# Attention row maxima from two heads side by side in 64-row tiles, with exps and outputs taken by halves of the queries

## The chip, the cores and the metric

The kernel runs on one core of one Trainium2 chip. A core has a matrix engine (TensorE, PE in the rows), a vector engine (DVE), a scalar engine (ACT), a general engine (GpSimd, POOL) and a sync engine (SP) that here issues DMAs. Each engine works through its own list of instructions in order and waits on semaphores that the others raise. The metric is the device time of the whole program in microseconds (us), the median of several runs; lower is better.

## The reference, cut to what matters

Two layers run over 4 batches of 1024 tokens of width 256: expert feed-forward, causal softmax attention, expert feed-forward, quantized feed-forward, linear attention, quantized feed-forward. The change is in the softmax attention, with 16 heads of width 16:

```python
qkv = (x @ W_qkv.T).reshape(B, L, 3, H, dk)      # B=4, L=1024, H=16, dk=16
attn = jnp.einsum('bhqd,bhkd->bhqk', q, k) * scale
attn = jnp.where(causal, attn, -jnp.inf)
attn = jax.nn.softmax(attn, axis=-1)
y = jnp.einsum('bhqk,bhkd->bhqd', attn, v)
```

## The kernel before, in words

`attention_phase` runs 16 iterations, one for each batch and group of four heads. q and k were written to DRAM as three bf16 parts each (high, middle, low), so that sums of part products come close to fp32. `load_block` reads them back as stacks: `sq` and `sk` hold, for each head, six blocks of 16 rows (96 rows, `SROWS`). Block r multiplies part `QROWS[r]` of q with part `KROWS[r]` of k, and one matmul over the 96 rows adds all six products:

```python
QROWS, KROWS = (0, 0, 1, 1, 0, 2), (0, 1, 0, 1, 2, 0)
```

Every score is computed twice.

- S pieces (`score_s`, L1351): queries on the partitions, keys along the row, over 96 rows. They serve for the row maxima alone. On the diagonal a second matmul (L1357, 128 rows) adds a large negative number where the key lies after the query. DVE takes the maximum over each piece (`reduce`, L1429). A piece fills at most one PSUM bank of 512 columns, and `psS` is a ring of three banks.
- E pieces (`score_e`, L1373): keys on the partitions, queries along the row, over 98 rows: 96 of the stack, and two that hold the negated maximum as two bf16 parts in `sq` against ones in `sk`. ACT takes the exponential into `PT` (L1485), POOL clears the triangle of the diagonal tile (L1332), and `weigh` (L1389) multiplies `PT` with the values in fp32, four heads in four 32-column tiles of the array, into `psO` (two banks). ACT copies `psO` out by halves (L1493), PE turns it (L1404), DVE divides.

An iteration has 38 S pieces and 38 E pieces. Each kind covers 4608 columns in each head, 18432 in all. The masks of the diagonal cover another 4096.

The order is written out by hand in `order`: E pieces go by key tile (`kt`), each over both halves of the queries; after every E piece stands one S piece of the next iteration, nine pieces ahead (`LEAD`). `weigh` of a key tile comes three pieces after its last E piece, so there are eight in an iteration. Ahead of the loop stand all S pieces of the first iteration and nine of the second. When the last S piece of an iteration has been reduced, DVE negates and splits the maxima, PE turns them (L1397), DVE copies them to `maxT` (L1451), and SP writes them into the spare rows of `sq` with two DMAs (L1295); the first E piece of the iteration waits for these. SP also loads the stacks two iterations ahead, with 12 DMAs of 128 KB each (L959).

Of the kernel before, what the change touches and what calls it, by code (L numbers as in the profile page):

```python
# [13 lines left out]
BF16 = mybir.dt.bfloat16  # L14
# [674 lines left out]
def experts(nc, st, sem, tag, ctx, r, psT, psH, psY, fp4=None, ring=TILES):  # L689
# [136 lines left out]
    def vector(dve):  # L826
# [30 lines left out]
        def set_spare_rows(t, p):  # L857

            if t < len(st.sk):
                dve.memset(st.sk[t][SROWS:P, :, :], 1.0)  # L860
# [328 lines left out]
def attention_phase(nc, st, sem, tag):  # L1189
# [5 lines left out]

    names = "s_filled s_drained e_filled e_drained maxed weighted o_out inverted v_set padded cleared spared".split()
# [3 lines left out]
    KROW = SROWS + 2  # L1200
    MAX = 4
    RING = 3
    LEAD = 9
    LAG = 3
    HALF = BT // 2

    s_pieces = []
# [6 lines left out]
    for kt in range(BT):  # L1214
        for c in range(kt // HALF, 2):
            n = (c + 1) * 512 - max(kt * P, c * 512)
            e_pieces += [(kt, c, n, h, 512 // n) for h in range(0, HG, 512 // n)] if n != 384 else \
                        [(kt, c, n, h, 1) for h in range(HG)]
    S, E = len(s_pieces), len(e_pieces)
    assert S == E  # L1220
    last_diagonal = [max(j for j, piece in enumerate(e_pieces) if piece[:2] == (kt, kt // HALF)) for kt in range(BT)]
    last_e = [max(j for j, piece in enumerate(e_pieces) if piece[0] == kt) for kt in range(BT)]
    turn_slot = S - 1 - LEAD + 3

    def order(it):

        if it < 0:
            for u in range(S + LEAD):
                yield "s", u // S, u % S
                if u == S + 2:  # L1230
                    yield "max", 0, 0
            return
        for j in range(E if it < ITS else 8):
            if it < ITS:
                yield "e", it, j
            u = (it + 1) * S + LEAD + j
            if u < ITS * S and it < ITS:
                yield "s", u // S, u % S
            if j == turn_slot and it + 1 < ITS:
                yield "max", it + 1, 0  # L1240
            for kt in range(BT):
                due = last_e[kt] + LAG
                if due < E and j == due and it < ITS:
                    yield "weigh", it, kt
# [1246 lines left out]
```

## Time and profile before

| what | value |
| --- | --- |
| median of 3 runs | 2176.65 us (2174.5 to 2178.46) |
| profiled execution, whole | 2175.08 us |
| profiled execution, span | 2173.4 us |
| PE / DVE / ACT / POOL busy | 2031.1 / 1467.3 / 1018.7 / 922.0 us |
| attention | about 437 to 937 us of the span |

The span is the time between the first and the last instruction of one profiled execution; 1.7 us of that execution lie outside it. Attention takes some 500 us of it. In the middle of that stretch the work of one iteration repeats exactly, so that a difference for one iteration can be multiplied by the number of iterations. The recorded length of a matmul includes the time that its results take to leave the array; the distance between the starts of neighbouring matmuls tells what one costs.

### The profile page before, as it was taken

The numbers are of one execution on the slowest core, as the hardware profiler recorded it, in microseconds if no ns is written. First come the engines' busy times: TensorE is split into PE (matmuls) and PEld (weight loads), VectorE is DVE, ScalarE is ACT, GpSimd is POOL, SyncE is SP. The second block draws the span as 40 slices with busy tenths as digits, with TensorE's granted clock in tenths as the row PEclk, the third lists the DMA queues.
The fourth block names the chain that finished last, engine by engine and source line by source line (L and its number), as shares of the span: only waits on it lengthen the run. The fifth ranks groups of instructions, "written<-read, shape, count | busy, mean of one in ns | idle before, by whom it ended". The sixth has DMA issues, their size and how long they took to land.

```text
span 2173.4 us, 41823 instructions
## 1 busy us (share of the span) xinstructions
PE 2031.1 (93%) x13717; PEld 1414.7 (65%) x13717; DVE 1467.3 (68%) x4020; ACT 1018.7 (47%) x2367; POOL 922.0 (42%) x1139
## 2 busy tenths in 40 slices
PE   6899999899999999977899998999989999799998
PEld 5899996534444444357799995666756666566676
DVE  4443555388888888535775358989866666588884
ACT  4333333336666666743433333333346666433332
POOL 4323655421111111214323555555556666455553
PEclk9899999969999999998999999999999999999999
DMA  5456663544443444012456652000000000000000
GB/s 185 172 193 213 229 211 119 164 59 60 60 50 50 51 60 60 2 41 95 161 184 213 234 187 51 0 0 0 1 1 2 2 2 2 2 11 17 12 20 20
DMA packets 101710, 173.58 MB, mean 80 GB/s; under 512 B 14704, under 2 KB 66320, under 8 KB 101520
## 3 DMA queue, kind: packets, MB, share of 16 engines
q1 hardware_dynamic: 95376, 154.40, 27.0%
q0 software_dynamic: 6144, 16.79, 2.4%
q8 instruction: 102, 1.67, 0.3%
q14 instruction: 88, 0.72, 0.1%
HBM read 136.01 MB, written 34.87 MB: 79 GB/s over the span
## 4 chain that ended last, share of the span: by engine, by line
PE 35%; DVE 11%; issue 5%; POOL 2%; ACT 2%; DVEq 0%; DMA 0%; POOLq 0%; SPq 0%; ACTq 0%
PE s_HH L785 5%; PE s_Y L797 4%; PE s_Y L1851 4%; PE s_R L1821 3%; PE s_HH L1821 3%; PE s_HH L2173 3%; PE s_R L2160 1%; PE s_R L452 1%; PE s_R L2208 1%; PE s_Y L2244 1%; PE s_Y L2252 1%; PE s_R L2194 1%; DVE ff_hscale L1534 1%; DVE fw_down L1537 1%; DVE s_HH L1714 1%
## 5 line engine op out<-in xcount | busy, mean ns | idle before, releaser
L1429 DVE TENSOR_REDUCE a_part_max<-a_psS 128x1 f32<-128x512 f32 (+3 forms) x608 | 362.6, 654 | 76.2 <-PE a_psS L1357 67.5
L1485 ACT ACTIVATE a_PT<-a_psE 128x512 f32<-128x512 f32 (+1 forms) x608 | 309.3, 584 | 175.9 <-PE a_psE L1373 159.0
L1332 POOL TENSOR_SCALAR_AFFINE_SELECT a_PT<-a_PT 128x512 f32<-128x512 f32 x128 | 81.2, 634 | 399.0 <-ACT a_PT L1485 399.0
L1764 POOL TENSOR_TENSOR fw_down<-fw_down,ff_hm 128x704 f32<-128x704 f32 x64 | 97.3, 1520 | 250.3 <-DVE fw_down L1546 250.3
L1851 PE MATMUL s_Y<-w_down,fw_up 128*128 128x256 f32 x768 | 181.0, 386 | 22.6 <-ACT fw_up L1801 20.9
L1786 ACT ACTIVATE ff_hm<-fw_down 128x704 bf16<-128x704 f32 x64 | 50.6, 790 | 279.7 <-DVE fw_down L1537 279.7
L1851 PEld LDWEIGHTS s_Y<-w_down,fw_up 128*128 128x128 f32 x768 | 143.7, 191 | 47.5 <-ACT fw_up L1801 30.5
L1821 PE MATMUL s_R<-w_gate,ff_xqT 128*128 128x512 f32 (+1 forms) x512 | 164.6, 465 | 4.8 <-ACT ff_sil L1796 4.8
L1821 PE MATMUL s_HH<-w_up,ff_xqT 128*128 128x512 f32 (+1 forms) x512 | 163.0, 462 | 3.6 <-DVE fw_down L1537 2.4
L1389 PE MATMUL a_psO<-a_PT,a_va 128*32 128x512 f32 (+3 forms) x1536 | 150.4, 494 | 2.5 <-POOL a_PT L1332 1.8
L1351 PE MATMUL a_psS<-a_sk,a_sq 96*128 96x512 bf16 (+2 forms) x480 | 144.0, 335 | 1.9 <-DVE a_part_max L1429 0.3
L1373 PE MATMUL a_psE<-a_sq,a_sk 98*128 98x512 bf16 (+3 forms) x480 | 140.6, 328 | 0.0
L785 PE MATMUL b_H<-e_xsT,e_w 128*128 128x128 f32 x1120 | 136.3, 281 | 0.0
L1821 PEld LDWEIGHTS s_R<-w_gate,ff_xqT 128*128 128x128 f32 x512 | 90.1, 193 | 67.4 <-issue 67.3
L797 PE MATMUL s_Y<-wo_moe,e_gT 128*128 128x256 f32 x560 | 129.2, 384 | 4.4 <-DVE e_y L844 2.5
L785 PE MATMUL s_HH<-e_xsT,e_w 128*128 128x128 f32 x1120 | 133.3, 278 | 0.0
L785 PEld LDWEIGHTS b_H<-e_xsT,e_w 128*128 128x128 f32 x1120 | 133.1, 198 | 0.1
L1821 PEld LDWEIGHTS s_HH<-w_up,ff_xqT 128*128 128x128 f32 x512 | 89.3, 191 | 66.0 <-issue 61.4
L785 PEld LDWEIGHTS s_HH<-e_xsT,e_w 128*128 128x128 f32 x1120 | 130.3, 195 | 0.1
L797 PE MATMUL b_Y<-wo_moe,e_gT 128*128 128x256 f32 x560 | 127.8, 381 | 0.0
L797 PEld LDWEIGHTS s_Y<-wo_moe,e_gT 128*128 128x128 f32 x560 | 104.9, 193 | 17.8 <-issue 2.7
L1990 POOL TENSOR_SCALAR_AFFINE_SELECT V<-V 128x512 f32<-128x512 f32 x128 | 78.0, 643 | 88.2 <-ACT V L2129 88.2
(484 smaller groups left out, 4308.6 us busy)
## 6 DMA issues: line engine op xcount, KB each, us to landing
e_w<-w_in SPq DMA_DIRECT2D x70, 1024.0 KB, 5.0
e_xs<-sorted_x SPq DMA_DIRECT2D x70, 128.0 KB, 3.5
e_xr<-sorted_x SPq DMA_DIRECT2D x70, 128.0 KB, 4.4
sorted_y<-e_yo SPq DMA_DIRECT2D x70, 128.0 KB
a_sq<-qk_parts SPq DMA_DIRECT2D x60, 128.0 KB, 6.5
a_sk<-qk_parts SPq DMA_DIRECT2D x60, 128.0 KB, 7.1
sq<-qk_parts SPq DMA_DIRECT2D x36, 128.0 KB, 5.8
sk<-qk_parts SPq DMA_DIRECT2D x36, 128.0 KB, 6.4
```

The lines of the kernel that those rows point to most:

```text
L785: mm = pe.matmul(psH[half][:, n * P:(n + 1) * P], w1[p][:, k, c * P:(c + 1) * P], xsT[p][:, k, :], start=k == 0, stop=k == KD - 1)
L797: mm = pe.matmul(psY[:, 0:D], gT[p][:, k, :], st.wo_moe[:, k, :], start=k == 0, stop=k == KI - 1, skip_group_check=True)
L1332: pool.affine_select(out=hidden, in_=hidden, compare_op=ALU.is_ge, fill=0.0, base=0, pattern=[[0, HG], [1, P]], channel_multiplier=-1).the ...
L1351: mm = pe.matmul(out[:, i * n:(i + 1) * n], sq[it % 3][0:SROWS, h0 + i, qt * P:(qt + 1) * P], sk[it % 3][0:SROWS, h0 + i, c * 512:c * 512 ...
L1373: mm = pe.matmul(out[:, i * n:(i + 1) * n], sk[it % 3][0:KROW, h0 + i, kt * P:(kt + 1) * P], sq[it % 3][0:KROW, h0 + i, q0:q0 + n], start= ...
L1389: mm = pe.matmul(psO[32 * h:32 * h + 32, q0:(c + 1) * 512], va[it % 2][:, kt, h, :], PT[kt % 2][:, h, q0:(c + 1) * 512], start=kt == 0, st ...
L1429: dve.tensor_reduce(part_max[:, c, h0:h0 + heads, qt], psS[place % RING][:, 0:heads * n].rearrange("p (h k) -> p h k", h=heads), AX.X, ALU ...
L1485: act.activation(PT[kt % 2][:, h0:h0 + heads, q0:q0 + n], psE[e % RING][:, 0:heads * n].rearrange("p (h q) -> p h q", h=heads), ACT.Exp, s ...
L1764: c.link(pool.tensor_tensor(hv[i], hv[i], hm[i][:], ALU.subtract))
L1821: mm = pe.matmul(out[:, a:b], xqT[p % 2][:, k, :], w[:, k, a:b], start=k == 0, stop=k == KD - 1)
L1851: mm = pe.matmul(psY[:, 0:D], hqT[p % 2][:, k, :], st.w_down[:, k, :], start=k == 0, stop=k == KF - 1)
L1990: pool.affine_select(out=a, in_=a, compare_op=ALU.is_ge, fill=0.0, base=0, pattern=[[0, 4], [1, P]], channel_multiplier=-1).then_inc(clear ...
```

## The change

- The stack is laid out anew for heads 2 and 3 of a group. Heads 0 and 1 keep their blocks in rows 0 to 95. Heads 2 and 3 have blocks 0 to 3 in rows 64 to 127 and blocks 4 and 5 in rows 32 to 63; their two rows of maxima are rows 0 and 1, and rows 0 to 31 are otherwise zeros in `sq` against ones in `sk`. Each DMA of a block is split in two (24 of 64 KB in an iteration), and so is each DMA of maxima (four of them).
- S pieces use blocks 0 to 3 alone, 64 rows: head h in rows 0 to 63, head h + 2 in rows 64 to 127, each with a matmul of its own, into two neighbouring banks. An iteration has 20 S pieces of up to 1024 columns, one DVE maximum goes over both banks, and `psS` is a ring of two pairs. The masks still use 128 rows.
- E pieces go by half of the queries (c) and then by key tile, and there are 12 groups of them (4 for the first half, 8 for the second). `weigh` is done for each group, 12 in an iteration, into one output bank that both halves use in turn. `PT` is a ring of four half-width tiles. E pieces of heads 2 and 3 are over 128 rows.
- An S piece is placed where the width of the E pieces so far calls for it (`s_due`), five pieces ahead.

```diff
+def stack_row(half, r):
+    return (r if half == 0 else r + 4 if r < 4 else r - 2) * HD
...
-        sp.dma_start(stack[it % 3][r * HD:(r + 1) * HD, :, :], src).then_inc(st.stacked[it % 3], 16)
+        for half in (0, 1):
+            row, heads = stack_row(half, r), slice(2 * half, 2 * half + 2)
+            sp.dma_start(stack[it % 3][row:row + HD, heads, :], src[:, heads, :]).then_inc(st.stacked[it % 3], 16)
...
-    RING = 3
-    LEAD = 9
+    PAIRS, RING, WEIGHTS = 2, 3, 4
+    LEAD = 5
...
-            s_pieces += [(qt, c, n, h, 512 // n) for h in range(0, HG, 512 // n)] if n != 384 else \
-                        [(qt, c, n, h, 1) for h in range(HG)]
+            s_pieces += [(qt, c, n, 0, 2)] if n <= 256 else [(qt, c, n, h, 1) for h in (0, 1)]
+    groups = [(c, kt) for c in (0, 1) for kt in range(HALF * (c + 1))]
...
+                for k in range(due[j - 1] if j else 0, due[j]):
+                    u = (it + 1) * S + LEAD + k
+                    if u < ITS * S:
+                        yield "s", u // S, u % S
...
-                for i in range(heads):
-                    mm = pe.matmul(out[:, i * n:(i + 1) * n],
-                                   sq[it % 3][0:SROWS, h0 + i, qt * P:(qt + 1) * P],
-                                   sk[it % 3][0:SROWS, h0 + i, c * 512:c * 512 + n],
-                                   start=i == 0, stop=not diagonal, skip_group_check=True)
+                for i in range(per):
+                    for half in (0, 1):
+                        rows, head = slice(64 * half, 64 * half + 64), 2 * half + h + i
+                        mm = pe.matmul(out[:, half, i * n:(i + 1) * n],
+                                       sq[it % 3][rows, head, qt * P:(qt + 1) * P],
+                                       sk[it % 3][rows, head, c * 512:c * 512 + n],
+                                       start=i == 0, stop=not diagonal, skip_group_check=True)
...
-                for c in range(kt // HALF, 2):
-                    q0 = max(kt * P, c * 512)
-                    for h in range(HG):
-                        mm = pe.matmul(psO[32 * h:32 * h + 32, q0:(c + 1) * 512], va[it % 2][:, kt, h, :],
+                q0 = max(kt * P - c * 512, 0)
+                for h in range(HG):
+                    mm = pe.matmul(psO[32 * h:32 * h + 32, q0:512], va[it % 2][:, kt, h, :],
...
-                dve.tensor_reduce(part_max[:, c, h0:h0 + heads, qt],
-                                  psS[place % RING][:, 0:heads * n].rearrange("p (h k) -> p h k", h=heads),
+                dve.tensor_reduce(part_max[:, c, :, qt].rearrange("p (b h) -> p b h", b=2)[:, :, h:h + per],
+                                  psS[place % PAIRS][:, :, 0:per * n].rearrange("p b (h k) -> p b h k", h=per),
```

PE's list before, in the middle of an iteration, between two `weigh`s (`a_psO`). `a_psE` are E pieces, `a_psS` S pieces, and `ident_bf` marks the mask:

```order
L1389 MATMUL a_psO<-a_PT0,a_va1 32x512 x4
L1373 MATMUL a_psE2<-a_sq2,a_sk2 128x512
L1351 MATMUL a_psS2<-sk0,sq0 128x512
L1357 MATMUL a_psS2<-hide_k_after_q,ident_bf 128x128
L1373 MATMUL a_psE0<-a_sq2,a_sk2 128x512
L1351 MATMUL a_psS0<-sk0,sq0 128x512
L1357 MATMUL a_psS0<-hide_k_after_q,ident_bf 128x128
L1373 MATMUL a_psE1<-a_sq2,a_sk2 128x512
L1351 MATMUL a_psS1<-sk0,sq0 128x512
```

The same place in the changed kernel, where L1409 is the E piece, L1385 the S piece and L1392 the mask:

```order
L1428 MATMUL a_psO<-a_PT2,a_va0 32x512 x4
L1409 MATMUL a_psE2<-sq0,sk0 128x512
L1385 MATMUL a_psS0<-a_sk1,a_sq1 128x512 x2
L1392 MATMUL a_psS0<-hide_k_after_q,ident_bf 128x128 x2
L1409 MATMUL a_psE0<-sq0,sk0 128x512
L1409 MATMUL a_psE1<-sq0,sk0 128x512
L1385 MATMUL a_psS1<-a_sk1,a_sq1 128x512 x2
L1392 MATMUL a_psS1<-hide_k_after_q,ident_bf 128x128 x2
L1409 MATMUL a_psE2<-sq0,sk0 128x512
```

An S piece is now two matmuls over 64 rows each (`x2`), and it stands between matmuls over 98 or 128 rows. Most have an E piece ahead of them and an E piece or a mask behind.

The second place is where the four `weigh`s of one half of the queries come close together. Before, around the last two `weigh`s of an iteration:

```order
L1389 MATMUL a_psO<-a_PT0,a_va1 32x256 x4
L1373 MATMUL a_psE2<-sq0,sk0 128x512
L1351 MATMUL a_psS1<-a_sk1,a_sq1 128x512
L1389 MATMUL a_psO<-a_PT1,a_va1 32x128 x4
L1373 MATMUL a_psE0<-sq0,sk0 128x512
L1351 MATMUL a_psS2<-a_sk1,a_sq1 128x512
```

Now, in the first half of the queries of an iteration, a place that had no counterpart:

```order
L1428 MATMUL a_psO<-a_PT1,a_va0 32x384 x4
L1409 MATMUL a_psE2<-sq0,sk0 128x512
L1385 MATMUL a_psS1<-a_sk1,a_sq1 128x512 x2
L1409 MATMUL a_psE0<-sq0,sk0 128x512
L1428 MATMUL a_psO<-a_PT2,a_va0 32x256 x4
L1409 MATMUL a_psE1<-sq0,sk0 128x512
L1385 MATMUL a_psS0<-a_sk1,a_sq1 128x256 x4
```

Such a run of narrow `weigh`s now comes twice in an iteration, once for each half.

## Rows read from the trace of the kernel before

**Rows 1.** The page: busy time of each engine; the span in 40 slices.

```profile
PE 2031.1 (93%) x13717; PEld 1414.7 (65%) x13717; DVE 1467.3 (68%) x4020; ACT 1018.7 (47%) x2367; POOL 922.0 (42%) x1139
PE   6899999899999999977899998999989999799998
```

**Rows 2.** Stretches of attention: us, busy of each engine, PE clock, DMA share.

```profile
449.00:453.00 4.00, 4.00 (x12) 1.04 (x11) 4.00 (x8) 0.00 (x0) 0.00 (x0) 0.50 0.40 46
620.00:680.00 60.00, 59.64 (x452) 25.40 (x450) 49.51 (x96) 40.83 (x83) 11.26 (x18) 1.00 0.46 55
925.00:930.00 5.00, 4.28 (x33) 1.09 (x25) 0.00 (x0) 3.69 (x8) 0.19 (x2) 1.00 0.00 2
```

**Rows 3.** Timeline, DVE: the copy of the maxima, one in an iteration.

```profile
609.85 0.20 DVE L1451 COPY a_maxT<-a_psS 64x128 bf16<-64x128 bf16 x1
639.51 0.20 DVE L1451 COPY a_maxT<-a_psS 64x128 bf16<-64x128 bf16 x1
```

**Rows 4.** Timeline, PE: an S piece and an E piece of 512 columns.

```profile
624.89 0.38 PE L1351 MATMUL a_psS<-sk,sq 96*128 96x512 bf16 x1
625.11 0.38 PE L1373 MATMUL a_psE<-a_sq,a_sk 98*128 98x512 bf16 x1
```

**Rows 5.** Timeline, PE: two `weigh`s (1024 and 640 columns a head) and their neighbours.

```profile
621.43 0.39 PE L1351 MATMUL a_psS<-sk,sq 96*128 96x512 bf16 x1
621.75 1.92 PE L1389 MATMUL a_psO<-a_PT,a_va 128*32 128x512 f32 x16
623.61 0.34 PE L1373 MATMUL a_psE<-a_sq,a_sk 98*128 98x384 bf16 x1
...
636.33 1.28 PE L1389 MATMUL a_psO<-a_PT,a_va 128*32 128x128 f32 x16
637.55 0.39 PE L1373 MATMUL a_psE<-a_sq,a_sk 98*128 98x512 bf16 x1
```

**Rows 6.** Timeline, PE and its weight loads: between 128 rows and 48.

```profile
1066.45 0.23 PE L593 MATMUL s_R<-r_numbers,ones_bf 128*128 128x128 bf16 x1 [3.11 <-DVE r_match_bf L640]
1066.61 0.23 PE L594 MATMUL s_R<-r_match_bf,r_numbers 48*128 48x128 bf16 x1
1066.77 0.70 PE L797 MATMUL s_Y<-wo_moe,e_gT 128*128 128x256 f32 x2
...
1061.27 0.10 PEld L588 LDWEIGHTS s_R<-r_diagonals,ones_bf 128*128 128x128 bf16 x1
1061.27 1.88 PEld L785 LDWEIGHTS s_HH<-e_xsT,e_w 128*128 128x128 f32 x16
```

**Rows 7.** Timeline, PE: linear attention, four 32-row tiles side by side, and fp32 transposes.

```profile
1699.96 0.41 PE L2278 MATMUL s_HH<-ident,e_gT 128*128 128x128 f32 x2 [0.21 <-issue]
1700.29 1.15 PE L2160 MATMUL s_R<-e_w,e_gT 32*128 32x256 f32 x16
1701.37 1.98 PE L2173 MATMUL s_HH<-lin_w,e_gT 128*128 128x512 f32 x4
...
1705.14 0.60 PE L2218 MATMUL s_R<-ident,e_w 128*128 128x128 f32 x4
1705.58 0.60 PE L2230 MATMUL s_HH<-ident,V 128*128 128x128 f32 x4
```

**Rows 8.** DVE maxima: groups by shape (busy, mean ns, idle before), timeline of five.

```profile
L1429 DVE TENSOR_REDUCE a_part_max<-a_psS 128x1 f32<-128x512 f32 x384 | 241.7, 681 | 26.7 <-PE a_psS L1357 19.0 <-PE a_psS L1351 7.8
L1429 DVE TENSOR_REDUCE a_part_max<-a_psS 128x1 f32<-128x384 f32 x128 | 65.9, 547 | 30.2 <-PE a_psS L1357 30.2
...
443.38 3.07 DVE L1429 TENSOR_REDUCE a_part_max<-a_psS 128x1 f32<-128x512 f32 x5
```

**Rows 9.** Maxima: DMA issues, a pair of them on SP, the first E piece behind.

```profile
a_sq<-a_maxT SPq DMA_DIRECT2D x20, 8.0 KB, 1.9
463.07 1.30 SPq L1295 DMA_DIRECT2D sq<-a_maxT  x2
...
644.14 0.39 PE L1373 MATMUL a_psE<-sq,sk 98*128 98x512 bf16 x1
```

More of the change, by code:

```diff
@@ L1210, in attention_phase, with s_due @@
             n = min(512, (qt + 1) * P - c * 512)
-            s_pieces += [(qt, c, n, h, 512 // n) for h in range(0, HG, 512 // n)] if n != 384 else \
-                        [(qt, c, n, h, 1) for h in range(HG)]
+            s_pieces += [(qt, c, n, 0, 2)] if n <= 256 else [(qt, c, n, h, 1) for h in (0, 1)]
+    groups = [(c, kt) for c in (0, 1) for kt in range(HALF * (c + 1))]
     e_pieces = []
-    for kt in range(BT):
-        for c in range(kt // HALF, 2):
[L1216 to L1223, printed above, removed]
+    for c, kt in groups:
+        n = (c + 1) * 512 - max(kt * P, c * 512)
+        e_pieces += [(c, kt, n, h, 512 // n) for h in range(0, HG, 512 // n)] if n != 384 else [(c, kt, n, h, 1) for h in range(HG)]
+    S, E, GR = len(s_pieces), len(e_pieces), len(groups)
+    last_e = {g: max(j for j, piece in enumerate(e_pieces) if piece[:2] == g) for g in groups}
+    group_at = {g: i for i, g in enumerate(groups)}
+    s_width, e_width = [n * per for _, _, n, _, per in s_pieces], [n * heads for _, _, n, _, heads in e_pieces]
+    s_of = lambda k: s_width[(LEAD + k) % S]
+    turn_slot = S - 1 - LEAD + 2
+    def s_due(j):
+        share, k = sum(e_width[0:j + 1]) * sum(s_width) / sum(e_width), 0
+        while k < S and sum(s_of(i) for i in range(k + 1)) <= share + 1e-6:
+            k += 1
+        return k
+    due = [s_due(j) for j in range(E)]
+    assert due[-1] == S
     def order(it):
@@ L1235, in order @@
                 yield "e", it, j
[L1236 to L1244, printed above, removed]
-                elif due >= E and j == due - E and it > 0:
-                    yield "weigh", it - 1, kt
-            if j == last_e[HALF - 1] + LAG + 2 and it < ITS:
-                yield "out", it, 0
-            if j == last_e[BT - 1] + LAG - E + 2 and it > 0:
-                yield "out", it - 1, 1
-            if j == last_e[HALF - 1] + LAG + 5 and it < ITS:
-                yield "turn", it, 0
-            if j == last_e[BT - 1] + LAG - E + 5 and it > 0:
-                yield "turn", it - 1, 1
+                for k in range(due[j - 1] if j else 0, due[j]):
+                    u = (it + 1) * S + LEAD + k
+                    if u < ITS * S:
+                        yield "s", u // S, u % S
+                    if k == turn_slot and it + 1 < ITS:
+                        yield "max", it + 1, 0
+            for g in groups:
+                at = last_e[g] + LAG
+                if at < E and j == at and it < ITS:
+                    yield "weigh", it, g
+                elif at >= E and j == at - E and it > 0:
+                    yield "weigh", it - 1, g
+            for c in (0, 1):
+                for what, later in (("out", 1), ("turn", 4)):
+                    at = last_e[c, HALF * (c + 1) - 1] + LAG + later
+                    if at < E and j == at and it < ITS:
+                        yield what, it, c
+                    elif at >= E and j == at - E and it > 0:
+                        yield what, it - 1, c
     def whole():
@@ L1355, in score_s @@
                 if diagonal:
-                    at = out[:, 0:heads * n].rearrange("p (h k) -> p h k", h=heads)[:, :, n - P:n]
-                    mm = pe.matmul(at, st.ident_bf[:], st.hide_k_after_q[:].unsqueeze(1).broadcast_to([P, heads, P]),
-                                   start=False, stop=True, skip_group_check=True)
+                    for half in (0, 1):
+                        at = out[:, half, 0:per * n].rearrange("p (h k) -> p h k", h=per)[:, :, n - P:n]
+                        mm = pe.matmul(at, st.ident_bf[:], st.hide_k_after_q[:].unsqueeze(1).broadcast_to([P, per, P]),
+                                       start=False, stop=True, skip_group_check=True)
@@ L1359, in score_s @@
                 mm.then_inc(s_filled, 1)
             def score_e(it, j):
-                kt, c, n, h0, heads = e_pieces[j]
+                c, kt, n, h0, heads = e_pieces[j]
                 e = it * E + j
@@ L1456, in divide @@
                 dve.wait_ge(s_filled, place + 1)
[L1457 removed]
+                o = psS[place % PAIRS][:, 0, :].rearrange("p (t h w) -> p t h w", t=HALF, w=32)
                 dve.reciprocal(inverse[c][:], o[:, :, :, HD]).then_inc(inverted, 1)
```

107 lines of the change are left out of this document (59 added, 48 removed).

## The prediction, made before the changed kernel ran

> **What bounds the kernel now.** I read the page first. PE is busy 93% of the span and at 8 or 9 tenths in nearly every slice; DVE is at 68% [rows 1]. The change is inside attention, so the second view is the busy time by stretches. In the middle of attention PE is busy 59.64 us of 60, DVE 49.51, ACT 40.83, POOL 11.26, and PE's clock is granted in full [rows 2]. A busy PE is not a PE at its peak, so the third view is the timeline. One iteration lasts 639.51 - 609.85 = 29.66 us, from one copy of the maxima to the next [rows 3].
>
> What fills these 29.66 us I add up from the starts of neighbouring matmuls.
> - 512 bf16 columns cost 0.22 us from start to start [rows 4], in finer terms 512 / 2.4 GHz = 0.213. E pieces: 18432 columns, 36 x 0.213 = 7.7 us. S pieces: the same, 7.7. Masks: 4096 columns, 1.7.
> - `weigh` of 1024 columns a head takes 623.61 - 621.75 = 1.86 us and of 640 columns 637.55 - 636.33 = 1.22 [rows 5]. The difference, 0.64 us for 384 columns, is 0.213 for 128: four passes over each column, with the four heads side by side. 1024 columns are then 1.71 us, and 0.15 is left over. Ahead of it stands an S piece that needs 0.213 and has 0.32 [rows 5], so 0.11 more. Each `weigh` thus costs some 0.25 us beside its columns. Eight of them: 4608 x 4 / 2400 = 7.7 us, and 8 x 0.25 = 2.0.
> - Turning the output: eight fp32 transposes, four of which take 0.44 [rows 7], 0.9; the maxima 0.05.
>
> Sum 27.8. The other 1.8 us are small stalls of PE, for the most part on DVE: its maximum over 512 columns takes 0.598 us from start to start ((3.07 - 0.68) / 4), more than the 0.43 of an S and an E piece, and only the `weigh`s let it catch up [rows 8]. So PE bounds an iteration, with DVE close behind.
>
> **The change, part by part.** Per iteration, at the full clock.
>
> 1. S pieces over 64 rows, two heads at once. That two heads in different rows run together is to be seen in linear attention: 16 instructions of 256 fp32 columns (two passes each, 0.213 us) over 32 rows took 1701.37 - 1700.29 = 1.08 us, where one after the other would need 3.4 and four at a time 0.85 [rows 7]. For pairs: 7.7 -> 3.85, a gain of 3.85 us. The masks stay at 1.7, since both heads still need their columns.
>
> 2. What stands against it is the change of tile. Between a matmul over 128 rows and one over 48 the weight load doesn't go ahead: starts are 0.16 us apart both ways (1066.45, 1066.61, 1066.77) for 128 columns that need 0.053, so 0.107 each way. Between two matmuls over 128 rows the next load starts with the one before (both at 1061.27), and costs nothing [rows 6]. The 96 and 98 rows of today are of that second kind [rows 4]. The 64-row pieces stand in 20 places, and all are entered and left through another shape; two are followed by a `weigh`, which has paid for a change anyway. Price of one place: the two changes alone, 0.21 (below it, nothing, if 64 rows behaved as 96 do); with four tiles filled in turn, 0.25 at `weigh` [rows 5]; with 32-row fp32 tiles (0.33 - 0.21) + (1.08 - 0.85) = 0.35 [rows 7]. I take 0.25, because it is in the middle, and has several tiles to fill: 20 x 0.25 - 2 x 0.11 = 4.8 us. Bounds 4.0 and 6.8.
> The Trainium skill says the same of the change of tile (TensorEngine Tiling (Array Packing), Key Properties): changing the tiling mode, not just the tile, drains TensorE. It speaks against this change, since with it the pieces alternate between modes. The trace agrees for 48 and 32 rows; no row has exactly 64. By that rule the sum is as here; by the page's "up to 2x" alone it would be that of rival B.
>
> 3. Twelve `weigh`s for eight: 4 x 0.25 = 1.0 us more. The columns are the same.
>
> 4. DVE: the same columns, 18 instructions fewer. The means of 681 ns for 512 columns and 547 for 384 give 1.05 ns a column [rows 8]; 512 of them are 0.536, so 0.06 us goes with each instruction. DVE has 18 x 0.06 = 1.1 us less to do. Its ring holds two pairs of 1024 columns, in columns as much as today or a little more. PE's stalls of 1.8 us can fall to nothing or stay. Between two `weigh`s a piece of E, E and S is 0.43 + 0.21 + 0.25 = 0.9 us of PE, against 1.13 us of DVE (2 x 0.536 + 0.06): DVE is still the slower one there, though by less. I take 1.2 us of stalls.
>
> 5. The maxima go by four DMAs in place of two. Today the first E piece comes 644.14 - 639.51 = 4.6 us after the copy [rows 3, 9]; copy, two issues (1.30 us for a pair) and 1.9 us to landing make 3.4, so 1.2 us is to spare. Two more issues take 1.1 to 1.3, and the copy may stand behind one maximum of 1.13 us. What PE waits there lies between 0 and 1.2; I take 0.6. Everything on PE behind this E piece waits, S pieces too.
>
> 6. One output bank. The first `weigh` of a half waits until ACT has copied the half before. Between them PE has four or five E pieces and two S pieces (some 2 us), against one exp and the copy, some 0.6 each. Hidden; if not, 0.3 us twice an iteration, which is inside the range. ACT has 40.83 of 60 us to do [rows 2], and its work is the same. POOL also.
>
> 7. The stacks are loaded by 24 DMAs of 64 KB for 12 of 128, two iterations ahead: the same bytes, at 0.46 of the DMA engines [rows 2]. Hidden. Ahead of the loop DVE bounds PE (4.00 of 4.00 busy at half the clock) [rows 2]; 25 pieces for 47 save 22 x 0.06 = 1.3 us. The memsets of the spare rows are done by POOL in that time.
>
> Sum of an iteration: E 7.7, S 3.85, masks 1.7, `weigh` 7.7 + 12 x 0.25 = 10.7, turns 0.95, changes of tile 4.8, stalls 1.2, wait for the maxima 0.6: 31.5 us, against 29.66. That is 1.84 more, for the 15 iterations that hold both E and S pieces 27.6 us. The last has no S pieces: about 1 more, for its four `weigh`s. Ahead of the loop 1.3 less. Together +27. The profiled execution took 2175.08 us; 2202. It is 1.6 under the median of the runs, so I say 2203.
>
> **The rivals.**
>
> A, the forecast. The changes of tile and the added `weigh`s (5.8) eat more than the pair gains (3.85). Its own range: 0.21 and 0.35 for a place give 30.7 to 33.5 us an iteration, 2190 to 2234.
>
> B, the other side: no change of tile between 128 and 64 rows. A place then costs the filling of its second tile at most, for which I take half of a weight load, 0.05. Columns and `weigh`s of the sum above are 24.9 us, the places 1.0. DVE now needs 36 x 0.536 + 20 x 0.06 = 20.5 us for the maxima and some 2.4 for the rest, so that stalls stay near today's 1.8; the wait for the maxima stays at 0.6. Together 28.3 us, 1.36 less than today, 20 us in 15 iterations: 2155. It decides from the price of a place at which the gain is gone: 0.25 - 1.84 / 20 = 0.16 us. For it: no row has 64 rows, and the 96-row pieces run without a gap. Against it: four changes in a row between 128 and 48 rows, and those at 32. Chance 0.25.
>
> C, the pairs don't run side by side, or at a price like 0.4 a place. S stays at 7.7 with the changes on top: 3.85 more in an iteration, less the stalls of 1.2, which a slower PE hides: 2.65 x 15 = 40 on the forecast, 2243. Against it the four tiles at once in [rows 7]. Chance 0.08.
>
> D, the clock. Ahead of the loop PE is granted half its clock although it is busy 4.00 of 4.00, with every S piece waiting for DVE; in the loop, with matmuls end to end, it is granted the whole, and it keeps it at the end of attention, with 4.28 of 5 busy [rows 2]. In the changed loop a quarter of the time is changes of tile (4.8 + 3.0 of 31.5), so the rise from half the clock could come later. An iteration at half the clock costs the columns once more, 22 us. One such: 2225; all sixteen: some 2550. Chance 0.07, nearly all for the first.
>
> E, no difference: the terms cancel within 0.2%, 4 us. Chance 0.07.
>
> **The numbers.** A has 0.53. Slower by over 0.2% (about what a measurement of this kernel can tell from none) hold A, C and D: 0.68. Faster: B, 0.25. The same: 0.07. The range is to hold 8 in 10: the better half of B and the upper end of A with most of C, 2156 to 2242. A alone: 2190 to 2234.
>
> **What the profile after should show.** A period of 31 to 32 us between copies of the maxima. The S pieces of a pair starting together, or within 0.1 us. Around them weight loads that start only when the columns before have gone through, 0.1 us lost on either side; an E piece behind an E piece with none. DVE busy some 22 us of an iteration. A short wait of the first E piece on the maxima's DMA. The forecast is wrong if the load of a 64-row piece starts during the E piece before it (B), if the second head of a pair starts 0.2 us after the first (C), or if PE's clock is at half beyond the first few microseconds of the loop (D).

## The result

The changed kernel took 2193.22 us in the median of four runs (2188.8 to 2199.99), the kernel before, run beside it, 2177.47 (2174.5 to 2178.46, four runs). The ratio is 1.0076, with a 95% interval from 1.0063 to 1.009: slower by 15.75 us. The forecast was 2203. Its sign was right, and its step was too large: it had +27 us.

The profiled execution of the changed kernel is the longest of the four (2199.99 us), so that I compare iterations and stages, not whole spans. The page first, its busy times and the slices [rows 1]:

```profile
PE 2023.8 (92%) x13701; PEld 1374.7 (63%) x13749; DVE 1458.4 (66%) x3734; ACT 1029.0 (47%) x2367; POOL 926.0 (42%) x1143
PE   6899999889999999877899998999989999799998
PEclk9899999979999999988999999999999999999999
```

PE shows less busy time in a longer span. Its digit has fallen from 9 to 8 in the 9th and the 17th slice, where attention's loop begins and ends; in the middle tenths are too coarse. The stretches say it more finely [rows 2]: length, busy time of PE, weight loads, DVE, ACT, POOL, then PE's clock, DMA share and GB/s.

```profile
469.00:473.00 4.00, 3.66 (x20) 0.95 (x19) 3.13 (x3) 2.83 (x6) 0.64 (x1) 0.74 0.49 138
473.00:477.00 4.00, 4.00 (x40) 1.64 (x37) 2.83 (x4) 2.81 (x6) 2.25 (x4) 1.00 0.50 143
620.00:680.00 60.00, 56.83 (x442) 19.35 (x440) 46.81 (x58) 40.68 (x80) 10.76 (x18) 1.00 0.20 54
```

PE is busy 56.83 us of 60 where it was 59.64. DVE is busy 46.81, which makes 23.7 us in an iteration (24.5 before). The granted clock comes to its full level, 2.4 GHz, at about 471 us, and stays there to the end of attention. The stacks' many small DMAs have not cost anything that I can see: the DMA engines' share is 0.20, where it was 0.46.

One iteration, from one copy of the maxima to the next [rows 3], with what SP and PE do behind it [rows 9]:

```profile
647.32 0.20 DVE L1490 COPY a_maxT<-a_psS 64x128 bf16<-64x128 bf16 x1
647.55 2.41 SPq L1323 DMA_DIRECT2D sq<-a_maxT  x4
651.18 0.61 PE L1409 MATMUL a_psE<-sq,sk 98*128 98x512 bf16 x2 [0.24 <-DMA sq<-a_maxT]
...
677.75 0.20 DVE L1490 COPY a_maxT<-a_psS 64x128 bf16<-64x128 bf16 x1
```

It lasts 30.43 us (29.66 before). Four issues take 2.41 us where a pair took 1.30. The first E piece, 3.86 us behind the copy, found its maxima 0.24 us late here; in some iterations it is 0.8 to 1.7, and those last 31 to 31.9 us. Over the fifteen iterations from 463.46 to 922.66 the mean is 30.61 (29.48 before), and without the first and the last of them, which are of another length in every kernel, 30.69. Attention begins at 438.08 us and ends (first matmul of the next stage) at 955.8, where it began at 437.37 and ended at 939.25: it takes 15.8 us longer, and this is the difference of the medians too. Of these, 17.0 lie between the first and the last copy of the maxima; up to the first copy it is 0.1 less, and behind the last one 1.1 less. The other 8.3 us by which this profiled execution is longer lie behind attention, where the two programs are the same. That part took 1233 to 1242 us in the profiled executions of this document, so a difference of a few us between medians says less than one between periods.

The place of a 64-row piece, in the timeline of PE and its weight loads:

```profile
648.62 0.10 PEld L1385 LDWEIGHTS a_psS<-a_sk,a_sq 64*128 64x128 bf16 x2 [0.21 <-issue]
648.62 0.34 PE L1385 MATMUL a_psS<-a_sk,a_sq 64*128 64x384 bf16 x2
648.88 0.11 PEld L1392 LDWEIGHTS a_psS<-hide_k_after_q,ident_bf 128*128 128x128 bf16 x2 [0.17 <-issue]
648.89 0.29 PE L1392 MATMUL a_psS<-hide_k_after_q,ident_bf 128*128 128x128 bf16 x2
648.96 0.49 PEld L1409 LDWEIGHTS a_psE<-a_sq,a_sk 128*128 128x128 bf16 x6
649.01 0.61 PE L1409 MATMUL a_psE<-a_sq,a_sk 128*128 128x256 bf16 x6
649.55 0.39 PE L1385 MATMUL a_psS<-a_sk,a_sq 64*128 64x512 bf16 x2
649.87 0.29 PE L1392 MATMUL a_psS<-hide_k_after_q,ident_bf 128*128 128x128 bf16 x2
```

Two heads of 384 columns stand in one row of two matmuls, and what follows starts 0.27 us later: 384 columns at 2.4 GHz are 0.16, and 0.11 is left for the change of tile. With 512 columns it is 0.32, so 0.21 and again 0.11. The two heads do run side by side. The loads of the 64-row piece, and of the mask behind it, start with their own matmuls: they have gone ahead of nothing. The load behind a mask, for an E piece over 128 rows (648.96), goes ahead by 0.05 us. On the way in it is 0.11 too: the six E matmuls at 649.01 are 1024 columns, which need 0.43 us and have 0.54. So a place costs 0.215 us, the lower bound of the forecast's range, and the second tile costs nothing that adds to it.

DVE's side [rows 8], by shapes, between 560 and 800 us (busy, mean ns, idle before):

```profile
L1468 DVE TENSOR_REDUCE a_part_max<-a_psS 128x2 f32<-128x1024 f32 x95 | 113.3, 1222 | 32.2 <-PE a_psS L1392 16.0 <-PE a_psS L1385 15.6
L1468 DVE TENSOR_REDUCE a_part_max<-a_psS 128x2 f32<-128x768 f32 x30 | 27.4, 954 | 8.5 <-PE a_psS L1392 8.5
```

And the waits of that stretch, us in total, times, longest:

```profile
PEld a_psE L1409 <- ACT a_PT L1522: 31.3, 52, 0.8
...
DVE a_part_max L1468 <- PE a_psS L1385: 15.6, 24, 0.7
...
PEld a_psS L1385 <- DVE a_part_max L1468: 10.5, 36, 0.4
```

DVE waits for PE to fill a pair of banks, and PE waits for DVE to empty one: each holds the other up, and neither is busy all the time. How much of this is due to the banks standing in pairs, these rows don't tell.

### The profile page after: what moved, and what is told of

Its sections match the earlier page's. It is cut to its first block, busy times and chain, and to the rows that moved or that the text cites. A ratio compares the mean times of both kernels' runs of the same rounds, so it can differ in the third digit from the quotient of the medians.

```text
span 2198.2 us, 41804 instructions
## 1 busy us (share of the span) xinstructions
PE 2023.8 (92%) x13701; PEld 1374.7 (63%) x13749; DVE 1458.4 (66%) x3734; ACT 1029.0 (47%) x2367; POOL 926.0 (42%) x1143
## 4 chain that ended last, share of the span: by engine, by line
PE 36%; DVE 10%; issue 5%; ACT 2%; POOL 2%; DMA 0%; DVEq 0%; POOLq 0%; SPq 0%; ACTq 0%
PE s_HH L785 5%; PE s_Y L797 5%; PE s_Y L1887 4%; PE s_HH L1857 3%; PE s_R L1857 3%; PE s_HH L2209 3%; PE s_R L452 2%; PE s_R L2196 1%; PE s_R L2244 1%; PE s_Y L2280 1%; PE s_Y L2288 1%; PE s_R L2230 1%; DVE ff_hscale L1570 1%; DVE fw_down L1573 1%; DVE s_HH L1750 1%
## 5 line engine op out<-in xcount | busy, mean ns | idle before, releaser
L1468 DVE TENSOR_REDUCE a_part_max<-a_psS 128x2 f32<-128x1024 f32 (+2 forms) x320 | 346.8, 1115 | 95.5 <-PE a_psS L1392 65.3
L1522 ACT ACTIVATE a_PT<-a_psE 128x512 f32<-128x512 f32 (+1 forms) x608 | 319.2, 579 | 181.5 <-PE a_psE L1409 176.5
L1428 PE MATMUL a_psO<-a_PT,a_va 128*32 128x512 f32 (+3 forms) x1536 | 163.6, 497 | 12.6 <-ACT a_PT L1522 5.3
L797 PEld LDWEIGHTS s_Y<-wo_moe,e_gT 128*128 128x128 f32 x560 | 105.7, 194 | 20.1 <-issue 4.0
L1409 PE MATMUL a_psE<-a_sq,a_sk 98*128 98x512 bf16 (+7 forms) x450 | 111.6, 326 | 4.9 <-DMA a_sq<-a_maxT 4.3
L821 ACT ACTIVATE e_gT<-b_H,e_bias 128x128 f32<-128x128 f32 x280 | 79.6, 369 | 77.0 <-PE b_H L785 77.0
```

The source lines that it names most:

```text
L797: mm = pe.matmul(psY[:, 0:D], gT[p][:, k, :], st.wo_moe[:, k, :], start=k == 0, stop=k == KI - 1, skip_group_check=True)
L821: ins = act.activation(gT[p][:, c, :], psH[half][:, n * P:(n + 1) * P], ACT.Gelu, bias=bias[p][:, c:c + 1])
L1409: mm = pe.matmul(out[:, i * n:(i + 1) * n], sk[it % 3][rows, h0 + i, kt * P:(kt + 1) * P], sq[it % 3][rows, h0 + i, q0:q0 + n], start=i == ...
L1428: mm = pe.matmul(psO[32 * h:32 * h + 32, q0:512], va[it % 2][:, kt, h, :], PT[(it * GR + group_at[g]) % WEIGHTS][:, h, q0:512], start=kt == 0,
L1468: dve.tensor_reduce(part_max[:, c, :, qt].rearrange("p (b h) -> p b h", b=2)[:, :, h:h + per], psS[place % PAIRS][:, :, 0:per * n].rearran ...
L1522: act.activation(PT[group % WEIGHTS][:, h0:h0 + heads, q0:512], psE[e % RING][:, 0:heads * n].rearrange("p (h q) -> p h q", h=heads), ACT.Exp,
```

## The experiments

Two things are to be told apart: what PE has to do by itself (columns, changes of tile, `weigh`s), and how long it stands because of the others. For each kernel I read the period in the middle of attention. PE's own work is the sum of the forecast, 27.8 us for the kernel before, with the terms that the runs below measured; the rest of the period I call stalls.

**x2_halves.** The kernel before, with only the other part of the change: exps by halves, four buffers of weights, twelve `weigh`s, one output bank. Score pieces as before.

```diff
-        PT = [sb(f"PT{i}", [P, HG, SEQ]) for i in (0, 1)]
+        PT = [sb(f"PT{i}", [P, HG, 512]) for i in range(WEIGHTS)]
...
-        psO = ps("psO", [P, SEQ])
+        psO = ps("psO", [P, 512])
...
-                for c in range(kt // HALF, 2):
-                    q0 = max(kt * P, c * 512)
+                q0 = max(kt * P - c * 512, 0)
```

> The kernel before with only the second part of the change: exps by halves of the queries, twelve weighs in place of eight, one output bank, PT as four half tiles. S pieces, ring and stacks as before. T: 4 more weighs at 0.25 us, 1.0 us an iteration, 2177 + 16 = 2193 (2188 to 2197). R: PE's stalls on DVE (1.8 us an iteration) absorb it: 2175 to 2182.

2182.62 us (ratio 1.0026, interval 1.0011 to 1.004): 0.6 above the rival's range and 5 below the theory's. The period is 29.82 us, 0.16 more than before:

```profile
641.76 0.21 DVE L1454 COPY a_maxT<-a_psS 64x128 bf16<-64x128 bf16 x1
671.58 0.21 DVE L1454 COPY a_maxT<-a_psS 64x128 bf16<-64x128 bf16 x1
```

Yet the four more `weigh`s do cost PE their price. A `weigh` of 512 columns takes 1.0 us from its start to the next, with 0.85 of columns, and the piece ahead of it has lost 0.1; that is the forecast's 0.25. PE's own work is 28.8 us. The stalls have fallen from 1.9 to 1.0. From 560 to 800 us the loads of the S pieces wait 20.1 us for DVE's maxima in the kernel before, and 10.3 us here. That this comes of the shorter `weigh`s, which hold up the others less, is my reading; no run varies it alone.

**x1_one_tile.** The changed kernel, its S pieces over 96 and 128 rows, one head after the other: no change of tile, nothing side by side; banks in pairs, maxima by four DMAs, order and halves as in the changed kernel. (A wait for the spare rows is added in iterations 1 and 2.)

```diff
...
-                        rows, head = slice(64 * half, 64 * half + 64), 2 * half + h + i
+                        rows, head = slice(0, SROWS if half == 0 else P), 2 * half + h + i
```

> The changed kernel, with its S pieces over 96 rows (heads 0 and 1) and 128 rows (heads 2 and 3) in place of 64, so that no tile is changed and the two heads of a pair run one after the other; order, banks and maxima as in the changed kernel. For heads 2 and 3 the extra rows add old maxima to the scores and the two low products. Theory T (a change of tile costs PE 0.107 us, 40 of them in an iteration, and that eats what the pairs gain): the pairs' 3.85 us an iteration come back as cost, the 4.1 of changes go, so within 5 us of the changed kernel's 2193: 2185 to 2197. Rival R (the changes are absorbed in waits for DVE; the loss comes from the ring of two pairs and the late maxima): nothing goes, 3.85 us an iteration are added, less what hides in stalls: 2225 to 2250.

2197.67 us (ratio 1.01, 1.0078 to 1.0121), just above the theory's range and far from the rival's. The period is 30.46, that of the changed kernel:

```profile
558.79 0.20 DVE L1492 COPY a_maxT<-a_psS 64x128 bf16<-64x128 bf16 x1
589.25 0.21 DVE L1492 COPY a_maxT<-a_psS 64x128 bf16<-64x128 bf16 x1
```

So the pairs side by side and their changes of tile, taken together, moved the period by nothing. And without either of them the kernel was already 0.8 us an iteration slower than before, 0.64 slower than x2_halves, which has the same work for PE. This I had not forecast. I had put the whole loss on the changes of tile and the added `weigh`s. In one period PE stands three times, for three others:

```profile
562.66 0.61 PE L1411 MATMUL a_psE<-sq,sk 98*128 98x512 bf16 x2 [0.22 <-DMA sq<-a_maxT]
585.16 0.39 PE L1387 MATMUL a_psS<-a_sk,a_sq 96*128 96x128 bf16 x4 [0.21 <-DVE a_part_max L1470]
588.57 1.06 PE L1430 MATMUL a_psO<-a_PT,a_va 128*32 128x512 f32 x8 [0.28 <-ACT a_PT L1524]
```

Together 0.71 us, where PE stands 0.11 in all in a period of x2_halves. One of the three is the wait for a pair of banks; the others are the maxima's DMA and a `weigh` that comes close behind its exps. x1_one_tile differs from x2_halves in the banks, in the order of the pieces and in the DMAs at once, so the 0.64 us are not divided among these by any run.

**x6_doubled.** The changed kernel with each S piece of more than 256 columns a head cut in two, an E piece between the parts: 16 more places, the same columns. Five of the new places are followed by a `weigh` and two stand behind one, which pays for a change anyway. Counted in the two lists, PE changes shape 87 times in an iteration where it did 62: 25 more.

```diff
+                lo, hi = (0, n) if per == 2 else (256, n) if second else (0, 256)
...
-                        mm = pe.matmul(out[:, half, i * n:(i + 1) * n],
+                        mm = pe.matmul(out[:, half, i * n + lo:i * n + hi],
```

> The changed kernel, with each S piece of 384 or 512 columns (16 of the 20) done in two parts, columns 0 to 255 and the rest, with an E piece between them: the same columns and maxima, some 14 to 16 more places where the tile is changed and changed back. T: 15 x 0.215 = 3.2 us an iteration, less up to 1 that hides in stalls: 2193 + 35 to 50 = 2228 to 2243. R: 2193 to 2205.

2246.16 us (ratio 1.033, 1.0311 to 1.0349), slightly above the range of the theory.

```profile
702.06 0.20 DVE L1509 COPY a_maxT<-a_psS 64x128 bf16<-64x128 bf16 x1
...
735.97 0.21 DVE L1509 COPY a_maxT<-a_psS 64x128 bf16<-64x128 bf16 x1
```

33.91 less 30.43 is 3.48 us. Of these, 25 changes at 0.107 are 2.7. The other 0.8 are waits: PE stands more for DVE's maxima in this period (0.58, 0.31 and 0.22 us) than in the changed kernel's (0.22).

```profile
713.20 0.29 PE L1400 MATMUL a_psS<-a_sk,a_sq 64*128 64x128 bf16 x4 [0.58 <-DVE a_part_max L1487]
723.13 0.28 PE L1400 MATMUL a_psS<-a_sk,a_sq 64*128 64x256 bf16 x2 [0.31 <-DVE a_part_max L1487]
```

3.48 over 16 places is 0.218 each, as if it were the timeline's 0.215 again, but this is a coincidence. What the run shows is that the price of a change of tile is real, that no stall absorbs it, and that it lies between 0.107 and 3.48 / 25 = 0.139 us. The Trainium skill has it as a drain when the tiling mode changes (TensorEngine Tiling (Array Packing), Key Properties). Forecast and rule stand, with 0.107 us each way at the full clock.

**x4_lead6** and **x0_mask_first.** The maxima's DMA, and the order inside a piece. The first starts the S pieces of an iteration one piece earlier (`LEAD = 6` for 5); the second adds the masks ahead of the scores, not behind them:

```diff
+                if diagonal and masks:
...
+                                  start=True, stop=False, skip_group_check=True)
-                                       start=i == 0, stop=not diagonal, skip_group_check=True)
+                                       start=i == 0 and not diagonal, stop=True, skip_group_check=True)
```

> The changed kernel with S pieces six ahead in place of five, so that the maxima are turned one piece (1.5 us) earlier against the first E piece. T: that piece no longer waits for the DMAs, 0.3 to 1.2 us an iteration: 2193 - 4 to 15 = 2178 to 2189, and the period is even at about 30.1. R (the wait only moves to DVE): 2190 to 2196.

> The changed kernel, with the mask of a diagonal piece written ahead of its scores and the scores added to it. The mask then joins the E piece before it, and the places at which the tile is changed stay as many. Theory T (0.107 us for each change of tile, on PE's path): the same as the changed kernel, a period of 30.4 us, 2188 to 2198. Rival R (what costs is the ring of two pairs, which the mask holds up): the same too; this run is the base of the next two.

x4_lead6: 2192.19 us (ratio 1.0078, 1.0061 to 1.0095), the rival. Every iteration lasts 30.47 us (30.1 had been expected), the uneven ones are gone, and the attention stage ends at 952.5, 3.3 us earlier than in the profiled execution of the changed kernel. The median moved by 1 us, within its uncertainty. Behind the first iteration no E piece waits for the maxima any more, but PE stands elsewhere, where it turns them:

```profile
612.52 0.23 PE L1436 MATMUL a_psS<-ident_bf,a_max_bf 128*128 128x128 bf16 x1 [0.75 <-DVE a_part_max L1468]
```

So the late maxima cost at most a few us. The forecast had 0.6 x 15 = 9. x0_mask_first, a single run, 2190.77 us: the period is 29.97 in its plain iterations (615.38 to 645.35), 0.46 less, and the stage ends at 950.8. The expectation had as many changes of tile as before, and that was wrong: with the masks ahead, six S pieces end in their scores right before a `weigh`, where two did, so PE changes shape 58 times for 62. Four changes are 0.43 us, which is nearly all of the 0.46.

**x3_twos**, **x5_by_weigh_l6**, **x5_by_weigh_l7.** If a change costs 0.107 us, fewer changes should pay. x3_twos emits the S pieces two by two, masks first, so that 42 changes of shape are left of 62. x5 holds the S pieces back to stand next to a `weigh`, which pays for a change anyway (37 and 36 are left), with a lead of 6 and of 7 pieces.

```diff
...
+            if w[0] == "s":
+                held.append(w)
+                if w[2] % 2 == 0:
+                    continue
+                yield from held
+                held = []
```

> As the run before, with S pieces two by two: the masks of both, then the scores of both, and six ahead in place of five. PE changes shape 42 times in an iteration in place of 62. T: 20 x 0.107 = 2.1 us an iteration less, of which 0 to 0.5 comes back as waits for DVE, which gets its work in bursts: a period of 28.3 to 28.9 us, 2162 to 2172. R: waits for DVE take it all, 2185 to 2200.

> As the run before, but S pieces are held back until the next weigh and stand right ahead of it, one or two at a time, so that the change out of the 64 rows is the one that the weigh needs anyway. PE changes shape 36 times in an iteration in place of 62. T: 26 x 0.107 = 2.8 us less, 0 to 1.0 of it lost to bursts on DVE: a period of 27.7 to 28.7 us, 2152 to 2170. R: 2185 to 2200. Another way to go wrong: held back, the maxima come late, and the first E piece waits for them, up to 1.5 us an iteration.

> The same with S pieces seven ahead. If the maxima were late in the run before, this one is faster by what PE waited for them there, up to 1.5 us an iteration; if not, the same within 3 us.

All three came out slower than the changed kernel: 2230.02 us (1.0247, 1.0212 to 1.0282), 2212.45 (1.0158, 1.0141 to 1.0175) and 2215.9 (1.017, 1.0153 to 1.0187). Theory and rival both missed for the first two; the third is no faster than the second, so late maxima were not what held that one up. The period of x3_twos is 32.21 us, with 20 changes fewer. Its timeline shows where they went:

```profile
694.33 0.82 PE L1421 MATMUL a_psE<-sq,sk 98*128 98x512 bf16 x3
695.60 0.38 PE L1395 MATMUL a_psS<-hide_k_after_q,ident_bf 128*128 128x256 bf16 x2 [0.44 <-DVE a_part_max L1487]
696.64 0.39 PE L1395 MATMUL a_psS<-hide_k_after_q,ident_bf 128*128 128x256 bf16 x2 [0.66 <-DVE a_part_max L1487]
...
698.11 0.23 PE L1448 MATMUL a_psS<-ident_bf,a_max_bf 128*128 128x128 bf16 x1 [0.64 <-DVE a_part_max L1487]
```

Two pieces in a row need both pairs of banks free at once, and DVE, at 1.22 us a pair, has not emptied the second. Then E pieces follow for which nothing waits, and DVE stands. Two more things lengthen this kernel. Up to the first copy of the maxima, where only S pieces are done, it needs 33.7 us of attention for 25.4 in the changed kernel. And four of its fifteen iterations last 33.4 us, not 32.21: at the start of each the granted clock is down at its lower level, 1.2 GHz, for 3.4 us, as from 665.4 on here, after PE had been busy 1.09 of 2 us.

```profile
663.00:665.00 2.00, 1.09 (x15) 0.54 (x19) 1.86 (x7) 0.00 (x0) 0.00 (x0) 1.00 0.00 0
665.00:668.00 3.00, 2.95 (x13) 0.56 (x14) 0.94 (x2) 1.04 (x3) 0.38 (x1) 0.57 0.02 3
```

This turned my attention to the ring: two pairs of banks.

**x7_halves_s4** and **x8_halves_e4.** The test of the ring. One output bank has set a bank free, and the changed kernel spends it on a second bank of a pair. Here it goes to x2_halves: as a fourth single bank for the maxima's scores (x7), or for those that the exps read (x8).

```diff
-    RING, WEIGHTS = 3, 4
+    SRING, RING, WEIGHTS = 4, 3, 4      (x8: 3, 4, 4)
...
-        psS = [ps(f"psS{i}", [P, 512]) for i in range(RING)]
+        psS = [ps(f"psS{i}", [P, 512]) for i in range(SRING)]
```

> The kernel before with the exps by halves and one output bank (as x2_halves), the freed bank given to the scores for the maxima: a ring of four single banks in place of three. Theory (ring): the iteration is stretched by PE and DVE waiting for each other through the few banks for the maxima's scores, and the kernel after made that worse by having two pairs of banks where before had three banks. Then a fourth bank takes stalls away: x2_halves' 29.82 us per iteration falls to 29.2-29.6, and the time from 2182.6 to 2168-2177 us. Rival (PE's own sum): the iteration is PE's work, the ring is no limit: as x2_halves, 2180-2185 us.

> As x7_halves_s4, but the freed bank goes to the ring of the scores that the exps read (four in place of three), and the maxima's ring keeps three. Theory (ring): DVE's banks are what stretches the iteration, ACT's are not: as x2_halves, 2179-2184 us. Rival (ACT's halves of exps are what PE waits for): up to 0.5 us per iteration comes back, 2172-2178 us.

x7: 2172.14 us (ratio 0.998, 0.9969 to 0.999). x8: 2176.94 (1.0008, 0.9999 to 1.0017). x8's period is x2's, 29.8 us (641.95 to 671.76), though its median is below the range of the theory, at the upper end of the rival's; the ratios of x2 and x8 differ by 0.0018, 3.9 us, of which their periods show nothing. Their profiled executions are 6.5 us apart, 1.0 in attention and 5.7 behind it, where the programs are the same. x7's period is 0.57 less:

```profile
634.96 0.21 DVE L1454 COPY a_maxT<-a_psS 64x128 bf16<-64x128 bf16 x1
...
664.20 0.21 DVE L1454 COPY a_maxT<-a_psS 64x128 bf16<-64x128 bf16 x1
```

The busy times of 620 to 680 us, as above, in x7:

```profile
620.00:680.00 60.00, 60.00 (x460) 25.49 (x459) 50.43 (x97) 41.70 (x82) 11.11 (x18) 1.00 0.47 57
```

PE is busy 60.00 us of 60, and DVE does more in it than in any other kernel. From 560 to 800 us the loads of x2's S pieces wait for DVE's banks 41 times (10.3 us); in x7 that wait is gone. The bank for the maxima was the one that was short, and not the bank for the exps. The list of waits alone would have picked the other one. For x2_halves it has:

```profile
PEld a_psE L1373 <- ACT a_PT L1486: 38.4, 56, 0.8
PEld a_psS L1351 <- DVE a_part_max L1432: 10.3, 41, 0.4
```

A load that waits costs nothing as long as its matmul still starts on time. At the E pieces behind a `weigh` the next start comes 0.145 us after the columns whether the list names ACT or nobody; at the S pieces at 653.50 and 671.12 of x2_halves it comes 0.09 and 0.24 us after them. x7 is the only kernel here that beats the one before, by 0.2%.

**x9_light** and **x10_twos_light.** The other side of the same question: leave the ring as it is, and halve DVE's work. x9 is made from the changed kernel, x10 from x3_twos.

```diff
-                                  psS[place % PAIRS][:, :, 0:per * n].rearrange("p b (h k) -> p b h k", h=per),
+                                  psS[place % PAIRS][:, :, 0:per * n].rearrange("p b (h k) -> p b h k", h=per)[:, :, :, 0:n // 2],
```

> The kernel after, but the maximum reads only the first half of each piece's columns, so that DVE takes about 0.6 us a piece in place of 1.13; half of the scores are left out of the row maxima, all else is done as in the kernel after. Theory (ring): the pairs of banks come free earlier, the stalls of PE go, and the iteration falls from 30.43 to PE's own sum of 29.0-29.4 us: 2193 less 15 to 21, 2171-2179 us. Rival (all of the 30.43 us is PE's own cost with the changes of tile): unchanged, 2189-2195 us.

> x3_twos (score pieces two by two, about 20 changes of tile fewer in an iteration) with the maximum over the first half of each piece's columns as in x9_light. Theory (ring): x3_twos was slow because two pieces at once leave PE waiting for DVE; with DVE's part halved the fewer changes show, 20 x 0.107 = 2.1 us per iteration under x9_light: 27.0-27.8 us per iteration, 2140-2155 us. Rival (grouping the pieces costs PE by itself, by bursts or its order): stays at 2200 us or above.

x9: 2178.68 us (ratio 1.0015, 1.0005 to 1.0026), 14.5 less than the changed kernel: in the theory's range, at its upper end. But this is partly luck. The period is 29.84, 0.59 less, not the 29.0 to 29.4 expected, and 15 x 0.59 is 9 us. Another 6.4 us are saved ahead of the loop, which the expectation didn't count: the first copy of the maxima comes 19.0 us into attention for 25.4, since DVE sets the pace there (4.00 us of 4.00 busy [rows 2]).

```profile
667.59 0.21 DVE L1490 COPY a_maxT<-a_psS 64x128 bf16<-64x128 bf16 x1
...
697.43 0.21 DVE L1490 COPY a_maxT<-a_psS 64x128 bf16<-64x128 bf16 x1
```

x10: 2186.75 us (1.0047, 1.0031 to 1.0062). With DVE's work halved 43 of x3_twos' some 53 extra us are gone, so most of its loss was DVE: 28 in the periods, 10 ahead of the loop, and 5 of the lower clock, which stays full here. But it stays at 30.33 us an iteration (671.57 to 701.90), slower than x9 with its twenty more changes, where I expected 2140 to 2155. Neither theory nor rival held. Part of the answer is in the rows:

```profile
692.90 0.29 PE L1395 MATMUL a_psS<-hide_k_after_q,ident_bf 128*128 128x128 bf16 x2 [0.48 <-DVE V L1518]
...
701.45 0.23 PE L1448 MATMUL a_psS<-ident_bf,a_max_bf 128*128 128x128 bf16 x1 [0.38 <-DVE a_part_max L1487]
...
703.68 0.34 PE L1421 MATMUL a_psE<-a_sq,a_sk 128*128 128x384 bf16 x1 [0.36 <-ACT a_PT L1541]
...
712.00 1.06 PE L1440 MATMUL a_psO<-a_PT,a_va 128*32 128x512 f32 x8 [0.30 <-POOL a_PT L1374]
```

With a fifth of this kind (0.43 us for V) PE stands 1.95 us in an iteration. I read it so: the results of the others come in the same rhythm as before, while PE now arrives in bursts; no run tests this. 1.95 is nearly the 2.14 that the changes were to save. How the rest is shared out (its sum leaves some 1.5 us unnamed) stays open.

## Why the prediction came out as it did

The accounts of the middle iterations, in us. Own work of PE: for the kernel before the forecast's sum; four more `weigh`s +1.0; side by side -3.84 (9216 columns fewer); 38 changes of tile beside those of the `weigh`s (20 places, two followed by a `weigh`), 0.107 each, so +4.1; x10 and x3 have 20 changes fewer. "Stalls" is what is left, whatever it is.

| kernel | period | own work | stalls |
|---|---|---|---|
| before | 29.66 | 27.8 | 1.9 |
| x2_halves: halves alone | 29.82 | 28.8 | 1.0 |
| x7_halves_s4: and four banks | 29.24 | 28.8 | 0.4 |
| x1_one_tile: halves, pairs of banks | 30.46 | 28.8 | 1.7 |
| after: and side by side | 30.43 | 29.0 | 1.4 |
| x9_light: and DVE halved | 29.84 | 29.0 | 0.8 |
| x10_twos_light | 30.33 | 26.9 | 3.4 |
| x3_twos | 32.21 | 26.9 | 5.3 |

In x7's rows no matmul starts late, and yet 0.4 is left. The sum has 0.213 us for 512 columns, the rows 0.22, so some 0.4 us of every line are not stalls at all. The differences between the lines are hardly touched by this.

The time was forecast well: 2193 for 2203, the right sign, inside the narrow range too. Of the signs written down, the pair that starts together, the loads and the short wait came as said; the period (30.4 for 31 to 32 us) and DVE's busy time (23.7 for some 22) did not.

Step 1, pairs side by side, -3.85: right. Two heads of 512 columns take the time of one.

Step 2, changes of tile, +4.8: the mechanism was right, the size was off. Measured 4.1. I had taken 0.25 for a place, the middle, because several tiles at once have to be filled; for two 64-row tiles that filling doesn't show, and the price is that of the two changes alone. It was written down as the lower bound. This is 0.7 of the 0.8 by which the sum of 31.5 exceeded the mean of 30.69.

Step 3, four `weigh`s, +1.0: right for PE's own work. By itself it moved the period by 0.16 only, since the stalls shrank beside it (x2). The forecast let the stalls shrink once for the whole change.

Step 4, stalls of 1.2: measured 1.4 in a plain iteration, 0.24 of which is the wait for the maxima that step 5 counts. But my reason was half a reason. I said that DVE's ring holds "in columns as much as today or a little more". It holds 2048 columns for 1536, but in two steps where there were three. The run that has the pairs without the tiles (x1) has 1.7 of stalls where x2, with the same work of PE and three banks, has 1.0, and four single banks have 0.4. By x1's rows the banks are one of three causes of that difference, beside the order and the DMAs. That the loss would be there without any change of tile was in none of the cases that I wrote down.

Step 5, the maxima's four DMAs, 0.6: right as a wait, too much as a cost. PE waits up to 1.7 us for them, 0.57 on the mean of the fifteen iterations. But with the wait gone (x4) the mean falls from 30.69 to 30.47 only, 0.2, since PE then stands for DVE.

Steps 6 and 7 (output bank, stacks): hidden, as forecast. The gain of 1.3 us ahead of the loop did not come (0.1), and the last iteration was 1.1 us shorter where 1 more was expected. The 24 DMAs of an iteration left no wait on PE that the trace shows outside of the maxima's.

Rival B asked for a price of a place under 0.16, and it is 0.215. C fell with the pairs that start together. D fell with the clock, which is full from 473 us on; only x3_twos shows the lower clock inside the loop, for 3.4 us at a time.

What decides against the change can be told in two ways. By accounts, PE's own work grows by 1.2 us, of which 0.5 come back in stalls. By runs, the halves add 0.16 us to the period, the banks in pairs with the order and the DMAs that come with them 0.64, and the pairs side by side with their changes of tile nothing (-0.03). The forecast had the last of these as the one that loses, 4.8 against 3.85. It only breaks even. That the sign still came out right is owed in good part to the 0.64, which the forecast did not have: there was luck in it. Had the freed bank gone to the ring instead, the halves alone would have cost 1.0 and given back 1.5.

## What to carry to other kernels

Halving the rows to run two heads side by side pays only when such pieces stand in long runs: here a place costs 0.215 us beside the others and saves on average 3.84 / 20 = 0.19. And long runs want banks: expect a grouping that saves one engine's changes to be paid back in waits (2.1 us saved, 3.9 lost). When two engines hand pieces over through a few banks, count the steps that the ring holds too, and not its columns alone; a fourth step was worth 0.57 us an iteration here, but whether two pairs are worse than three single banks, all else equal, no run tells. When a bank comes free, the cheapest thing to try with it is one more step for the ring behind whose waits matmuls start late. Look at the starts for this, not at the sum of the waits.

## What the runs showed of the hardware that was not expected

- Two 64-row tiles (bf16, 512 columns a head) run side by side without any stagger: the pair takes the 0.213 us of one, beside the changes. In linear attention sixteen matmuls over 32-row tiles, four side by side, took 1.08 us for 0.85 of columns [rows 7].
- The change of tile costs some 0.107 us each way between 64 and 128 rows, the same as between 48 and 128 [rows 6]. 96, 98 and 128 rows mix at no price, in x1 too.
- A `weigh` has 0.145 us beside its columns whatever its length (128, 256, 384 and 512 columns a head take 0.36, 0.57, 0.785 and 0.995 us in x7), and the piece ahead of it loses some 0.10.
- A mask of 128 or 256 columns may open a bank's accumulation ahead of the scores at no extra cost to PE (x0_mask_first): the one run of it was faster by 0.46 us an iteration, 0.43 of which are its four changes of shape fewer.
- A granted clock that is full can fall for 3.4 us to 1.2 GHz in the middle of the loop (x3_twos: at four of fifteen iterations, each 1.15 us longer for it).
